# Attention: pairs of key blocks added by GpSimd before the ones product, and the stores moved one group forward

## The reference

```
x = x + tanh(g_xattn) * (softmax(Q K^T / sqrt(32)) V Wo^T + bo)
        Q = layernorm(x) Wq^T + bq;  K, V = ctx Wk^T + bk, ctx Wv^T + bv
x = x + tanh(g_ffn) * experts(layernorm(x))
```

## Time and profile before

| | |
|---|---|
| median of three runs | 1820.79 us |
| the profiled execution | 1820.35 us |
| its span, first to last instruction | 1818.6 us |
| mean granted PE clock | 0.975 |
| PE busy | 1722.9 us (95%) |
| VectorE busy | 1077.2 us (59%) |
| ScalarE busy | 798.5 us (44%) |
| GpSimd busy | 435.4 us (24%) |

### The profile page before, as it was taken

How to read it: one execution, slowest core, us unless ns; L and a number is a source line. 1 busy time by engine, 2 the same in 40 slices (tenths; PEclk the granted TensorE clock), 3 DMA queues, 4 the chain that set the end, 5 groups by cost and what they waited for, 6 DMA issues and landing times.

```text
span 1818.6 us, 29436 instructions
## 1 busy us (share of the span) xinstructions
PE 1722.9 (95%) x10322; PEld 828.1 (46%) x10322; DVE 1077.2 (59%) x2087; ACT 798.5 (44%) x1092; POOL 435.4 (24%) x424
## 2 busy tenths in 40 slices
PE   7999999999999999999716999999999999999998
PEld 4324243342423334242304647465665747565563
DVE  6777867778776777867587625345352625434231
ACT  4563735546364554735322516153342616244240
POOL 2332434223333332421211121211121121112101
PEclk9999999999999999999956999999999999999999
DMA  6334263433425433343122553635253362626312
GB/s 225 106 77 132 72 164 114 103 121 98 140 93 143 134 93 116 90 112 99 47 94 82 140 138 100 161 86 158 73 163 90 105 160 86 177 49 177 77 45 28
DMA packets 214606, 203.17 MB, mean 112 GB/s; under 512 B 121812, under 2 KB 162912, under 8 KB 210456
## 3 DMA queue, kind: packets, MB, share of 16 engines
q1 hardware_dynamic: 193432, 181.80, 33.0%
q0 software_dynamic: 21120, 20.67, 6.4%
HBM read 134.57 MB, written 43.63 MB: 98 GB/s over the span
## 4 chain that ended last, share of the span: by engine, by line
PE 84%; DVE 9%; issue 3%; ACT 2%; POOL 1%; DMA 1%; SPq 0%; DVEq 0%; ACTq 0%; POOLq 0%
PE psum L1556 23%; PE psum L1532 21%; PE psum L1354 7%; PE psum L1361 6%; PE psum L1345 6%; PE psum L1335 6%; PE psum L1325 6%; PE psum L1447 4%; PE psum L1372 3%; DVE mx L925 2%; DVE reached L1077 1%; DVE x2hl L997 1%; DVE x2hl L999 1%; DVE stats L877 1%; DVE x2n L884 1%
## 5 line engine op out<-in xcount | busy, mean ns | idle before, releaser
L1556 PE MATMUL psum<-w,hT 128*128 128x512 f16 (+1 forms) x1920 | 415.7, 379 | 0.0
L1532 PE MATMUL psum<-xgT,w 128*128 128x308 f16 (+1 forms) x3072 | 409.7, 294 | 0.8 <-DVE xgT L1178 0.8
L925 DVE TENSOR_REDUCE mx<-psum 128x1 f32<-128x512 f32 x512 | 330.1, 683 | 105.6 <-PE psum L1335 104.0
L1532 PEld LDWEIGHTS psum<-xgT,w 128*128 128x128 f16 x3072 | 296.8, 97 | 110.2 <-DVE xgT L1178 1.1
L779 ACT ACTIVATE pt<-psum 128x1024 f32<-128x1024 f32 x256 | 255.1, 1022 | 116.3 <-PE psum L1345 116.3
L1556 PEld LDWEIGHTS psum<-w,hT 128*128 128x128 f16 (+1 forms) x1920 | 199.3, 104 | 213.8
L851 ACT ACTIVATE h<-psum,b1c 128x308 f32<-128x308 f32 (+1 forms) x256 | 118.1, 512 | 343.3 <-PE psum L1532 342.9
L1199 DVE TENSOR_TENSOR hT<-h,hT 128x615 f16<-128x615 f32 x128 | 102.5, 801 | 211.5 <-ACT hT L854 211.5
L672 POOL DMA_INDIRECT out_dram<-y,idx_now x40 | 88.0, 2201 | 498.4 <-DVE y L1231 311.7
L1228 DVE SCALAR_TENSOR_TENSOR y<-psum,b2b 128x512 f32<-128x512 f32 (+1 forms) x40 | 27.7, 692 | 270.1 <-PE psum L1556 270.1
L1325 PE MATMUL psum<-actT,wT 128*128 128x512 f16 x768 | 179.2, 381 | 2.0 <-DVE wT L912 2.0
(11 more groups left out here) (187 smaller groups left out, 1511.8 us busy)
## 6 DMA issues: line engine op xcount, KB each, us to landing
stage<-in_L_ffn_W_dram SPq DMA_DIRECT2D x62, 1024.0 KB, 5.8
stk<-qk_rows SPq DMA_DIRECT2D x192, 128.0 KB, 2.5
qk_rows<-qks SPq DMA_DIRECT2D x64, 256.0 KB, 2.5
xin<-in_x_dram SPq DMA_DIRECT2D x8, 1024.0 KB, 5.4
cin<-in_ctx_dram SPq DMA_DIRECT2D x8, 1024.0 KB, 7.6
xres<-in_x_dram SPq DMA_DIRECT2D x8, 1024.0 KB, 5.6
out_dram<-xres SPq DMA_DIRECT2D x32, 256.0 KB, 2.1
x_split<-x2hl SPq DMA_DIRECT2D x32, 256.0 KB, 2.3
```

Of the source, the lines that this page charges most:

```text
L925: v.reduce_max(mx[:, KT * t + qt:KT * t + qt + 1], ps, AX.X).then_inc(read, 1)
L1532: mm = t_.matmul(psum[:, (2 * m + ch) % 4, 0:c1 - c0], w1[:, wp, kt, m * P:(m + 1) * P], xgT[:, KT * xp + kt, c0:c1], start=(kt == 0 and ( ...
L1556: mm = t_.matmul(psum[0:rows, Y_BANK[i], :], hT[:, hp, k, c * P:c * P + rows], w2[:, wp, k, :], start=(k == 0 and (hp, wp) == (0, 0)), sto ...
```

## The change

1. Sums. For units 0 to 7 GpSimd adds the exponents of unit 2p + 1 onto those of unit 2p (four adds of 128x512 f32 a pair, four pairs), and the ones product is made of the pair. Units 8 to 15 keep a ones product each. `SUMS` says in which slot each is made: pairs in 10, 12, 14, 16, units in 17, 18 (two), 19, 20 (two), 21, 22. PE waits for a pair's adds (`pair_added`).
2. Order of a PE slot. In slots with scores the ones product, if there is one, takes the place of the values product, and the values product comes at the end.
3. Buffers. The exponents lie in five unit buffers, `pt` and three tiles that are free at that time; ScalarE waits until the sum over the unit five before is done (and, for the first five, for all of GpSimd's projection splits).
4. GpSimd's order. Behind the splits come the wait for `xres` and its four adds, then the four pairs. The inverse deviations for the next x move in front of the last two splits; the normalisation itself goes to VectorE, slots 5 and 6.
5. SyncE's order. `STORE_GROUP` is 0: stores and load of `xres` follow the first group's maxima rows and the stacking behind them.
6. Reciprocals. VectorE transposes the sums in 32x32 blocks, takes one reciprocal of the 16 distinct columns, and transposes them back with a broadcast. `GROUP_NORM` goes from 14, 17, 20, 23 to 16, 18, 20, 23, and ScalarE's split has slots of its own, 17, 19, 21, 23.

```diff
-STORE_GROUP = 1
+STORE_GROUP = 0
 GROUP_END = [LAG_C + 4 * g + 3 for g in range(NG)]
-RECIP_SLOT = ((11, 12, 13, 14), (15, 16, 16, 17), (19, 19, 20, 20), (23, 23, 23, 23))
-GROUP_NORM = [slots[-1] for slots in RECIP_SLOT]
+PAIRS, PT_UNITS = 4, 5
+SUMS = {10: (("pair", 0),), 12: (("pair", 1),), 14: (("pair", 2),), 16: (("pair", 3),), 17: (("unit", 8),),
+        18: (("unit", 9), ("unit", 10)), 19: (("unit", 11),), 20: (("unit", 12), ("unit", 13)),
+        21: (("unit", 14),), 22: (("unit", 15),)}
+SUM_ORDER = [term for slot in sorted(SUMS) for term in SUMS[slot]]
+SUM_COUNT = len(SUM_ORDER)
+GROUP_SUMS = [[i for i, (kind, n) in enumerate(SUM_ORDER) if n // (2 if kind == "pair" else 4) == g] for g in range(NG)]
+SUMS_END = [max(slot for slot in SUMS for term in SUMS[slot] if SUM_ORDER.index(term) in GROUP_SUMS[g]) for g in range(NG)]
+GROUP_NORM = [16, 18, 20, 23]
+GROUP_SPLIT = [17, 19, 21, 23]
+X_NORM_SLOT = (5, 5, 6, 6)
...
+def sum_of_unit(u):
+
+    return SUM_ORDER.index(("pair", u // 2) if u < 2 * PAIRS else ("unit", u))
...
+        pt_units = ([pt[:, 2 * i:2 * i + 2, :, :] for i in range(2)]
+                    + [a.rearrange("p (a b) s -> p a b s", b=2) for a in (qk32[:, :, :], x2nT[:, :, :], x2n[:, :, :])])
...
                     if i == QK_FIRST + 2:
+                        if not last:
+                            for tt in range(KT - 1):
+                                inverse_deviation(0, tt, KT * b + (KT + tt))
                         pool.wait_ge(mrow_ready, NG * b + 1)
+                    if i == QK_FIRST + 3 and not last:
+                        inverse_deviation(0, KT - 1, KT * b + (2 * KT - 1))
                     pool.wait_ge(qk32_ready, NQ * b + i + 1)
                     copied(pool, use, ("qk", i), b)
                     g.tensor_tensor(qks[:, n, 1, m, :], qk32[:, i % 4, :], qks[:, n, 0, m, :],
                                     ALU.subtract).then_inc(qk_split, 1)
-                pool.wait_ge(mrow_ready, NG * b + 2)
-                if not last:
-                    for tt in range(KT):
-                        n = KT * b + (KT + tt)
-                        inverse_deviation(0, tt, n)
-                        pool.wait_ge(ln_rstd[0], n + 1)
-                        settle(pool)
-                        g.tensor_scalar(xn[:, tt, :], xin[:, tt, :], mv[:, 0, tt, 0:1], rstd[:, 0, tt:tt + 1],
-                                        ALU.subtract, ALU.mult).then_inc(xn_ready, 1)
-
-                pool.wait_ge(mrow_ready, NG * b + 3)
                 pool.wait_ge(xres_in, 16 * b + 16)
                 pool.wait_ge(tgbo_ready, 1)
                 for tt in range(KT):
                     g.tensor_tensor(xres[:, tt, :], xres[:, tt, :], tgbo[:, :], ALU.add).then_inc(xres_biased, 1)
+                for p in range(PAIRS):
+
+                    if p % 2 == 0:
+                        pool.wait_ge(mrow_ready, NG * b + (p // 2 + 2))
+                    pool.wait_ge(pv_done, UNITS * b + (2 * p + 1))
+                    for hf in range(2):
+                        copied(pool, use, ("ST", 2 * p + 1, hf), b)
+                        for j in range(2):
+                            into = pt_units[2 * p % PT_UNITS][:, hf, j, :]
+                            g.tensor_tensor(into, into, pt_units[(2 * p + 1) % PT_UNITS][:, hf, j, :],
+                                            ALU.add).then_inc(pair_added, 1)
...
-                            act.wait_ge(pv_done, UNITS * b + max(u - 1, 0))
+                            if u < PT_UNITS:
+                                act.wait_ge(sums_done, SUM_COUNT * b)
+                                act.wait_ge(qk_split, NQ * b + NQ)
+                            else:
...
-                def reciprocals(g, quarters):
+                def inverse_sums(g):
                     if g < NG - 1:
-                        dve.wait_ge(osum_ready, (NG - 1) * b + g + 1)
                         dve.wait_ge(sums_ready, (NG - 1) * b + g + 1)
                         sums = osum[:, g % 2, 1, :]
                     else:
 
-                        dve.wait_ge(pv_done, UNITS * b + UNITS)
+                        dve.wait_ge(sums_done, SUM_COUNT * b + SUM_COUNT)
                         dve.wait_ge(norm_done, NG * b + g)
                         sums = psum[:, 7, :]
-                    for i in quarters:
-                        v.reciprocal(osum[:, g % 2, 1, i * P:(i + 1) * P], sums[:, i * P:(i + 1) * P]).then_inc(rinv_done, 1)
+                    v.transpose(turned_sums[:, :], sums).then_inc(sums_turned, 1)
+                    dve.wait_ge(sums_turned, NG * b + g + 1)
+                    own = mx[:, NT // 2 * g:NT // 2 * g + NT // 2]
+                    v.reciprocal(own, turned_sums[:, :].rearrange("p (c k) -> p c k", k=32)[:, :, 0:1].rearrange(
+                        "p c k -> p (c k)")).then_inc(sums_inverted, 1)
+                    dve.wait_ge(sums_inverted, NG * b + g + 1)
+                    v.transpose(osum[:, g % 2, 1, :].rearrange("p (c k) -> p c k", k=32),
+                                own.rearrange("p (c o) -> p c o", o=1).to_broadcast((P, NT // 2, 32))).then_inc(rinv_done, 1)
...
+                def with_ones(s):
+                    for kind, n in SUMS.get(s, ()):
+                        i = SUM_ORDER.index((kind, n))
+                        terms = next(t for t in GROUP_SUMS if i in t)
+                        gr = GROUP_SUMS.index(terms)
+                        if i == terms[0] and gr > 0:
+                            pe.wait_ge(sums_ready, (NG - 1) * b + gr)
+                        if kind == "pair":
+                            pe.wait_ge(pair_added, 4 * PAIRS * b + (4 * n + 4))
+                        src = pt_units[(2 * n if kind == "pair" else n) % PT_UNITS]
                         for j in range(4):
-                            last = t_.matmul(psum[32 * j:32 * j + 32, 7, :], ones32[:, :],
-                                             pt[:, (2 * u + j // 2) % 4, j % 2, :], start=(kt == 0), stop=(kt == KT - 1))
-                        last.then_inc(pv_done, 1)
+                            last = t_.matmul(psum[32 * j:32 * j + 32, 7, :], ones32[:, :], src[:, j // 2, j % 2, :],
+                                             start=(i == terms[0]), stop=(i == terms[-1]))
+                        last.then_inc(sums_done, 1)
...
+                    if s < UNITS:
+                        with_ones(s)
+                        scores(s, 2)
+                    less_maxima(u, 1)
+                    scores(s, 3)
...
+                    with_values(s - LAG_C)
                     if s >= UNITS:
-                        less_maxima(u, 1)
-                        with_values(s - LAG_C)
-                    else:
-                        with_values(s - LAG_C)
-                        scores(s, 2)
-                        less_maxima(u, 1)
-                        scores(s, 3)
-                    if 0 < s - LAG_C < UNITS and (s - LAG_C) % 4 == 0:
-                        pe.wait_ge(sums_ready, (NG - 1) * b + (s - LAG_C) // 4)
-                    with_ones(s - LAG_C)
+                        with_ones(s)
                     filling(s, 1)
                 for gs in (range(KT - 1), range(KT - 1, KT)):
                     for tt in range(KT):
```

More of the change, by code:

```diff
@@ L157, in layer_kernel @@
         next_hl = [qks[:, n, :, :, :].rearrange("p a k s -> p (a k s)").rearrange("p (t d) -> p t d", t=KT) for n in range(2)]
+        turned_sums = stk[:, 0, 0:2, :].rearrange("p h s -> p (h s)").bitcast(f32)
         t32 = sb("t32", [P, S], f32)
@@ L334, in layer_kernel @@
         mrow_in = [sem(f"mrow_in{g}") for g in range(NG)]
-        pv_done = sem("pv_done")
-        osum_ready, sums_ready, rinv_done, norm_done, a32_ready, a_hi, a_ready = (
-            sem(n) for n in ("osum_ready", "sums_ready", "rinv_done", "norm_done", "a32_ready", "a_hi", "a_ready"))
+        pv_done, pair_added, sums_done = sem("pv_done"), sem("pair_added"), sem("sums_done")
+        osum_ready, sums_ready, sums_turned, sums_inverted, rinv_done, norm_done, a32_ready, a_hi, a_ready = (
+            sem(n) for n in ("osum_ready", "sums_ready", "sums_turned", "sums_inverted", "rinv_done", "norm_done", "a32_ready", "a_hi", "a_ready"))
         xres_biased, x1_stored = sem("xres_biased"), sem("x1_stored")
@@ L774, in batch @@
                         if 0 <= u < UNITS:
-                            act.wait_ge(pv_done, UNITS * b + max(u - 1, 0))
+                            if u < PT_UNITS:
+                                act.wait_ge(sums_done, SUM_COUNT * b)
+                                act.wait_ge(qk_split, NQ * b + NQ)
+                            else:
+                                act.wait_ge(sums_done, SUM_COUNT * b + (sum_of_unit(u - PT_UNITS) + 1))
                             bank, _ = use(("ST", u, hf), b)
                             _, read = filled(act, use, ("ST", u, hf), b)
-                            s.activation(pt[:, (2 * u + hf) % 4, :, :], psum[:, bank:bank + 2, :], ACT.Exp,
```

(37 more changed lines are left out.)

## The result

The changed kernel takes 1890.97 us (median of 4 runs, 1889.05 to 1893.83) against 1820.76 for the kernel before (4 runs, 1820.34 to 1822.04): a ratio of 1.0389, 95% interval 1.0373 to 1.0406. The profiled execution took 1889.05 us, its span 1887.3. Forecast were 1887 us and a range of 1867 to 1908.

A forecast was written before the change was run, and what follows sets the result against it. PE was taken to bound the kernel, busy for 95% of the span. Per batch +8.0 (wait) + 1.5 (clock) - 3 x 0.75 (slots) + 1.75 (tail) = +9.0; with the first batch's +3, +66 on 1820.8: 1887 us, range 1867 to 1908.

The forecast's parts named there:

- The load of xres: SyncE, second batch: load issued at 186.3, 9.3 us sooner, landing 5.6 us later (5.1 to 6.3), at 191.9.
- Adds: GpSimd: 4.96 us for four adds, to xres and per pair; pair 0 ready at 202.0, slot 10's middle 8.0 us later.
- The gain of slots 7 to 9 is swallowed: PE: the wait for pair 0 in slot 10 swallows the 2 us gained in slots 7 to 9.
- costs nothing beside what follows: SyncE: group 1's maxima rows, issued behind the load of xres, may land a little late for slot 10, at no cost.
- Clock: PE, slot 10: clock falls to 1.2 GHz 3.3 us into the wait, 3 us at half speed, 1.5 us lost (0 to 3.0).
- Slots: PE: a slot without a ones product lasts 3.2 us, a gain of 0.75 (0 to 1.0); with one, 3.94.
- Tail: PE, slots 16 to 22: two more ones products, nine in place of seven, cost +1.75 us a batch.
- Sum: Whole kernel: +9.0 us for each of batches 1 to 7, +63, and +3 for the first batch, together +66 us.
- VectorE at nothing: VectorE: normalisation and turned reciprocals are off the path and cost nothing; without the last group's cover, at most 2 us a batch.
- The first rival: GpSimd's pairs come in time, so PE doesn't wait: -2.75 us a batch, -22 us, 1799 us; chance 6%.

The follow-up runs named there:

- e1: The changed kernel with GpSimd's wait for xres and its four adds moved behind the four pairs: 1804.25 us, ratio 0.9914.
- e3: The changed kernel with only STORE_GROUP set back to 1, so stores and load of xres stand behind group 1's maxima rows: 1955.24 us, ratio 1.0736.
- e2: The kernel of e1 with STORE_GROUP set back to 1, so stores and load of xres stand behind group 1's maxima rows: 1797.44 us, ratio 0.9874.
- e6: The changed kernel with 39 filler matmuls a batch (22 in the first) on PE ahead of its wait for pair 0: 1873.46 us, ratio 1.0290.
- e8: The kernel of e2 with the old reciprocals of all 512 columns in four quarters, at the slot of the group's product: 1812.00 us, ratio 0.9948.
- e4: The changed kernel with 30 filler matmuls a batch (12 in the first) on PE ahead of its wait for pair 0: 1883.84 us, ratio 1.0345.
- e7: The kernel of e2 with units 8 and 9 as a fifth pair and the xres adds behind GpSimd's split of group 0: 1791.91 us, ratio 0.9844.

## Why the prediction was right

It was right in sign, in size (1887 against 1890.97) and in the mechanism. Step by step, with 2.47 us taken off the times of the second batch:

- *The load of xres.* Issue forecast 186.3, measured 188.81 - 2.47 = 186.34. Landing taken as 5.6 us, the median of before; GpSimd began 6.2 us after the issue, and the median of the eight is 6.0. Here 0.4 us a batch were missing.
- *Adds.* 4.96 forecast for four, 4.92 and 4.91 measured. Pair 0's product was forecast for 202.0, a move of 8.0 us, and came at 204.83 - 2.47 = 202.36, a move of 8.3. e1 shows that the order is the cause, e3 that the wait follows the load.
- *The gain of slots 7 to 9 is swallowed,* and so is the wait for the maxima rows: so it was. Without the wait for the pair the second of them shows, 6.8 us in all between e1 and e2; "costs nothing beside what follows" was right only beside it.
- *Clock.* 1.5 us a batch forecast, 1.85 measured (e6 against the changed kernel). The forecast took 3 us at half speed; PE ran 3.4 us at it in the second batch, and the rest of slot 10, which takes 2.97, took up to 5.6. A term sized too small, within its bounds. The clock fell 2.3 us into the wait and not 3.3; it had fallen either way before PE began again, so this cost the forecast nothing.
- *Slots.* 3.2 forecast without a product, 3.14 and 3.15 measured; 3.94 with one, as forecast.
- *Tail.* +1.75 forecast, 20.41 - 19.10 = +1.3 measured. A second product costs 0.86; and a wait of some 0.3 us for ScalarE's copy of a finished group, which the kernel before has in this stretch, is gone. A term too large, and it hid part of the two that were too small.
- *Sum.* +9.0 a batch forecast, 117.15 - 107.89 = +9.3 measured. The measured terms, 8.3 + 1.85 - 3 x 0.8 + 1.3, give +9.1; that the sum is closer than its clock and tail terms is luck, for their misses cancel. So it is in the first batch, +3 forecast and +2.5 measured: pair 0's product moved by 87.48 - 86.03 = +1.45 and not by +2.6, and the clock took 2.2 and not 1. From the start of the last output projection to the end 1.4 us more than before were not forecast and are not explained; e1 to e8 have between 0.1 and 2.3 more there.
- *VectorE at nothing.* Right for the change as it stands. The prediction named the cover of the last group alone; e8 shows that the groups before it have less cover than it thought, because ScalarE's exponents queue behind its split of the group.
- *The first rival* (1799 us if the pairs came in time, -2.75 a batch) did not come true for the change. Its time and its -2.75 a batch are what e2 measured, 1797.4 and -2.83, but not by its condition, an early load: there the pairs don't stand behind the load at all.

## What to carry to other kernels

Before work is put on an idle engine, write out its queue and the landing time of everything that it waits for in front of the new work: here 12 us more of GpSimd's work a batch cost 0.2 us of waiting at most (e2), and a wait for a load that stood ahead of them cost 87 us. An instruction that another engine waits for goes ahead of one that nobody needs until the end of the stage, on compute queues and on the DMA queue alike (e1 and e2). And a wait of the bounding engine is priced with the slow clock behind it, here 1.85 us on a wait of 9.

## What the runs showed of the hardware

The clock can fall after the wait is over. In e4 PE stood still for 2.17 us up to 206.56 and was then at work; the granted clock was 1.00 between 207 and 208 and 0.53 between 208 and 209, so it fell 1.5 us after PE had begun again. The rest of slot 10 was longer than its 2.97 us behind each of the eight waits of e4 (2.08 to 4.14 us) and behind none of the seven of e6 (0.30 to 1.05 us).

The adds of GpSimd, 1.27 us each, and the row reductions of VectorE from PSUM did not slow each other: four adds took 4.96 us beside the reductions (215.01) and 4.91 with VectorE idle (199.87), and two reductions took 1.34 us beside pair 3's adds (222.00) and 1.34 in the kernel before with GpSimd idle (183.65). The same adds beside VectorE's work on two operands in SBUF took 5.88 us for four (e7), and the four adds to xres, which also fall there in e7, took 6.34 (217.10); VectorE's product of a group took 1.23 us in place of 0.69.
